# Two-layer transformer kernel: self key scores without mask products, GpSimd zeroing of unseen exponentials, value products in halves between pairs of score steps

## What is computed

```python
w = jnp.einsum('bhqd,bhkd->bhqk', q, k) / jnp.sqrt(jnp.asarray(HD, q.dtype))
if causal_bool:                      # self attention
    mask = jnp.tril(jnp.ones((ql, kl), bool))
    w = jnp.where(mask[None, None], w, neg)
if tril_diag2_additive:              # cross attention: two keys further are seen
    cm = jnp.tril(jnp.ones((ql, kl), w.dtype), k=2)
    w = w + jnp.where(cm == 0, neg, jnp.zeros((), w.dtype))[None, None]
if extra_bias is not None:
    w = w + extra_bias[:, None, None, :]
w = jax.nn.softmax(w, axis=-1)
return jnp.einsum('bhqk,bhkd->bhqd', w, v)
```

## Time and profile before

| | |
|---|---|
| median of 3 runs | 1627.18 us (1626.68 to 1628.8) |
| the profiled execution's own time | 1632.07 us |
| its span | 1630.3 us |
| TensorE busy | 1429.8 us (88%) |
| VectorE busy | 1114.9 us (68%) |
| ScalarE busy | 987.3 us (61%) |
| GpSimd busy | 317.8 us (19%) |
| mean granted TensorE clock | 0.956 |

### The profile page before, as it was taken

One profiled execution on the slowest core, in us unless ns is written; L12 is line 12 of the kernel. 1 busy time (PEld: TensorE's weight loads), 2 busy tenths in 40 slices (PEclk: granted clock), 3 DMA queues, 4 the chain that ended last, 5 costly groups with the idle time before them and its releaser, 6 DMA issues. The chain is left out here.

```text
span 1630.3 us, 39092 instructions
## 1 busy us (share of the span) xinstructions
PE 1429.8 (88%) x15448; PEld 877.1 (54%) x15448; DVE 1114.9 (68%) x3252; ACT 987.3 (61%) x1618; POOL 317.8 (19%) x428
## 2 busy tenths in 40 slices
PE   2667799989899999989899999989899998989887
PEld 1445565655656465555646565555656565555442
DVE  5556676786777677777777677677767667646344
ACT  2254666675757576675757567585757666572642
POOL 3421211121212121121212111121212102020120
PEclk7587899999999999999999999999999999997998
DMA  3324111213040312213040222203031211010000
GB/s 70 57 74 58 44 33 39 38 32 50 12 71 10 54 29 38 38 25 57 10 73 10 46 30 38 45 19 63 10 62 21 38 32 35 2 32 5 14 7 7
DMA packets 79214, 58.05 MB, mean 36 GB/s; under 512 B 11004, under 2 KB 78902, under 8 KB 79030
## 3 DMA queue, kind: packets, MB, share of 16 engines
q1 hardware_dynamic: 76726, 53.90, 18.9%
q10 hardware_dynamic: 2304, 1.64, 0.7%
HBM read 11.57 MB, written 4.19 MB: 10 GB/s over the span
## 5 line engine op out<-in xcount | busy, mean ns | idle before, releaser
L1025 DVE TENSOR_REDUCE chunkmax<-ps 128x3 f32<-128x384 f32 (+1 forms) x1024 | 507.8, 553 | 116.7 <-PE ps L1379 111.1
L711 ACT ACTIVATE probs<-ps 128x768 f32<-128x768 f32 (+1 forms) x512 | 405.6, 808 | 183.5 <-PE ps L1374 179.8
L1444 PE MATMUL ps<-zT,w 128*128 128x512 f32 x576 | 281.5, 603 | 6.9 <-ACT silu_a L728 5.2
L728 ACT ACTIVATE silu_a<-ps,b 128x512 f32<-128x512 f32 x144 | 98.7, 685 | 198.2 <-PE ps L1444 174.8
L1359 PE MATMUL ps<-k_op,q_op 48*128 48x256 bf16 x512 | 145.2, 286 | 52.0 <-DVE chunkmax L1025 38.2
L1166 DVE SCALAR_TENSOR_TENSOR h_open<-ps,b,silu_a 128x512 f32<-128x512 f32 x128 | 95.7, 748 | 124.0 <-PE ps L1444 113.5
L1341 PE MATMUL ps<-q_op,k_op 51*128 51x256 bf16 x512 | 143.4, 280 | 27.1 <-DMA xq_op<-xq_parts 9.1
L1444 PEld LDWEIGHTS ps<-zT,w 128*128 128x128 f32 x576 | 103.0, 192 | 114.5 <-issue 87.3
L1480 PE MATMUL ps<-hT,w 128*128 128x512 f32 x288 | 149.5, 600 | 3.8 <-DVE hT L1172 3.0
L1359 PE MATMUL ps<-xk_op,xq_op 51*128 51x256 bf16 x512 | 145.3, 285 | 5.1 <-DVE chunkmax L1025 4.8
L1371 PE MATMUL ps<-xmask_q_lo,ident_lo 64*128 64x262 bf16 x512 | 145.1, 285 | 0.0
(11 more groups left out here) (245 smaller groups left out, 3436.4 us busy)
## 6 DMA issues: line engine op xcount, KB each, us to landing
q_op<-q_parts SPq DMA_DIRECT2D x192, 64.0 KB
xq_op<-xq_parts SPq DMA_DIRECT2D x192, 64.0 KB
k_op<-k_parts SPq DMA_DIRECT2D x168, 64.0 KB
x_tm<-in_L_attn_hidden_states SPq DMA_DIRECT2D x16, 256.0 KB, 6.0
x_keep<-in_L_attn_hidden_states SPq DMA_DIRECT2D x16, 256.0 KB, 6.1
out<-o_tm SPq DMA_DIRECT2D x16, 256.0 KB, 2.3
k_op<-k_parts ACTq DMA_DIRECT2D x24, 64.0 KB
w<-in_L_ffn_rw SPq DMA_DIRECT2D x1, 1024.0 KB
```

The costliest lines, as they stand in the source:

```text
L711: act.activation(probs[:, four % 2, 2 * pair:2 * pair + 2, 0:T + a.seen], ps[:, 2 * (1 - g % 2):2 * (1 - g % 2) + 2, 0:T + a.seen], ACT.Ex ...
L1025: dve.tensor_reduce(chunkmax[:, b, at, :], ps[:, MAX_BANK[n], 0:3 * a.seen].rearrange("p (c n) -> p c n", c=3), AX.X, ALU.max).then_inc(a. ...
L1444: pe.matmul(ps[:, bank, :], w, src[:], start=True, stop=True).then_inc(sig.sem, 1)
```

## The change

The self attention's key scores get no mask products any more (`first_keys`, `second_keys`; `a.selects` is true for the self attention). Behind each exponential GpSimd sets the unseen entries of its 128x(2x2x128) block to zero (`keep_seen`, `affine_select` in place) and raises a new semaphore `kept`, for which the value products of the self attention wait in place of `exp`. `probs` gets a third buffer, used by the self attention only, so its value products may come one group later. To make room, three weight tiles of the setup now lie in `geluT`.

A value group is cut into its two halves. In the self phase two steps are written out together (`two_steps`), and a half follows every second step: the first half of group g behind step 4g+9, its second half behind step 4g+11. Groups 6 and 7 come when all steps are done. In the cross phase `score_step` stays, the first half of group g comes behind step 4g+6 and the second behind step 4g+8, and groups 6 and 7 come at the end. The query scores that run beside self key scores use banks 6, 7, 5 until step 23, banks 6 and 7 for steps 24 to 27, and 4, 6, 7 from step 28 (`WITH_SELF`). By the rule (4, 6, 7)[n % 3] steps 28 and 29 fall into banks 6 and 7 too. ScalarE copies the first context half behind exponential 11 in place of 10 in the self phase.

```diff
-        mask_k_lo = sb("mask_k_lo", [128, 2, 64], BF16)
-        mask_k_hi = sb("mask_k_hi", [128, 256], BF16)
...
-        probs = sb("probs", [128, 2, 4, T + XW])
+        probs = sb("probs", [128, 3, 4, T + XW])
...
+        wxq0, wxk, wxkv = geluT[:, 3, 0:D], geluT[:, 3, D:2 * D], geluT[:, 3, 2 * D:4 * D]
...
+            a.selects = not cross
+            a.kept = signal(n + "_kept", H)
+            a.buffers = 2 if cross else 3
...
+        def max_banks(shared, own):
+            n_5, n_4 = shared, own
+            return [(6, 7, 5)[n % 3] for n in range(n_5)] + [(6, 7)[n % 2] for n in range(n_5, n_4)] \
+                + [(4, 6, 7)[n % 3] for n in range(n_4, 2 * H)]
+        WITH_SELF, WITH_CROSS = max_banks(24, 28), max_banks(20, 24)
+        def banks_for(a, j):
+            return WITH_SELF if a.cross or j < 2 else WITH_CROSS
...
-                for m in (mask_k_lo, mask_k_hi, xmask_q_lo, xmask_q_hi, xmask_k_lo, xmask_k_hi, pick):
+                for m in (xmask_q_lo, xmask_q_hi, xmask_k_lo, xmask_k_hi, pick):
...
-                    select(mask_k_lo[p], ALU.is_ge, MASKED, 0, [[0, 2], [1, 64]], -1)
-                    select(mask_k_hi[p], ALU.is_ge, MASKED, -HALF, [[0, 2], [1, 128]], -1)
...
+            def keep_seen(a, j, first, last):
+                for g in range(first, last):
+                    four, pair = divmod(g, 2)
+                    late_and_early = probs[:, four % a.buffers, 2 * pair:2 * pair + 2, 0:2 * a.seen]
+                    pool.wait_ge(*a.exp.part(j, g + 1))
+                    pool.affine_select(out=late_and_early, in_=late_and_early, compare_op=ALU.is_ge, fill=0.0, base=0,
+                                       pattern=[[0, 2], [0, 2], [1, a.seen]],
+                                       channel_multiplier=-1).then_inc(a.kept.sem, 1)
             def body(i, par):
                 k = i - 2
 
+                if exists(i):
+                    keep_seen(sa, i, 0, 2)
                 if exists(k):
 
                     pool.wait_ge(*n_mlp.out.done(k))
                     add_bias(h2b, h2, bmlp, ca.h.done(k), h3_sb.before(k), h2b_ready)
+                if exists(i):
+                    keep_seen(sa, i, 2, H)
...
-                    act.wait_ge(*(a.pv.part(j, four - 1) if four >= 2 else used_before))
+                    act.wait_ge(*(a.pv.part(j, four + 1 - a.buffers) if four >= a.buffers else used_before))
...
-                    if g == 10:
+                    if g == (10 if a.cross else 11):
...
+            def first_keys(a, j, par, m):
+                kt, qt, h2, k0, q0 = key_operands(a, par, m)
+                if m % 2 == 0 and m >= 4:
+                    pe.wait_ge(*a.exp.part(j, m // 2 - 1))
+                pe.matmul(bank_of(m)[:, a.seen:a.seen + T], kt[:, h2, k0:k0 + 128], qt[:, h2, q0:q0 + T],
+                          start=True, stop=False, skip_group_check=True)
+            def second_keys(a, j, par, m):
+                kt, qt, h2, k0, q0 = key_operands(a, par, m)
+                last = pe.matmul(bank_of(m)[:, 0:a.seen], kt[:, h2, k0 + 128:k0 + T], qt[:, h2, q0 + T - a.seen:q0 + T],
+                                 start=False, stop=a.selects, skip_group_check=True)
+                if a.selects and m % 2:
+                    last.then_inc(a.st_ps.sem, 1)
...
+                if keys and not a.selects:
+                    first_key_mask(a, m)
...
+            def two_steps(a, j, par, other, jo, paro, n, free_4, free_5):
+                first_keys(a, j, par, n)
+                late_queries(a, j, other, jo, paro, n, free_4, free_5)
+                second_keys(a, j, par, n)
+                early_queries(other, jo, paro, n)
+                late_queries(a, j, other, jo, paro, n + 1, free_4, free_5)
+                late_query_mask(other, jo, n)
+                early_queries(other, jo, paro, n + 1)
+                early_query_mask(other, jo, n)
+                first_keys(a, j, par, n + 1)
+                late_query_mask(other, jo, n + 1)
+                second_keys(a, j, par, n + 1)
+                early_query_mask(other, jo, n + 1)
...
+            def value_half(a, four, half, j, par):
 
                 s, b, aa = four // 4, four // 2 % 2, four % 2
-                pe.wait_ge(*a.exp.part(j, 2 * four + 2))
+                if half == 0:
+                    pe.wait_ge(*(a.kept if a.selects else a.exp).part(j, 2 * four + 2))
                 late = T - a.seen
                 bank = ps[:, 4 + s, :]
-                for half in range(2):
-                    for jj in range(4):
-                        h = 8 * s + 4 * aa + jj
-                        v = xv_st[:, half, h, :] if a.cross else v_st[:, par, 2 * b + half, h, :]
-                        q0 = b * T + (late if half else 0)
-                        last = pe.matmul(bank[32 * jj:32 * jj + 32, q0:(b + 1) * T], v,
-                                         probs[:, four % 2, jj, (0 if half else a.seen):(a.seen if half else a.seen + T)],
-                                         start=(aa == 0 and half == 0), stop=(aa == 1 and half == 1),
-                                         skip_group_check=True)
-                last.then_inc(a.pv.sem, 1)
+                for jj in range(4):
+                    h = 8 * s + 4 * aa + jj
+                    v = xv_st[:, half, h, :] if a.cross else v_st[:, par, 2 * b + half, h, :]
+                    q0 = b * T + (late if half else 0)
+                    last = pe.matmul(bank[32 * jj:32 * jj + 32, q0:(b + 1) * T], v,
+                                     probs[:, four % a.buffers, jj, (0 if half else a.seen):(a.seen if half else a.seen + T)],
+                                     start=(aa == 0 and half == 0), stop=(aa == 1 and half == 1),
+                                     skip_group_check=True)
+                if half:
+                    last.then_inc(a.pv.sem, 1)
+            def values_behind(a, j, par, other, jo, step, free_4, free_5):
+                four, at = divmod(step, 4)
+                lag = a.buffers - 1
+                first, second = (1, 3) if a.selects else (2, 4)
+                if at == second % 4 and four >= lag + second // 4:
+                    value_half(a, four - lag - second // 4, 1, j, par)
+                if at == first and lag <= four < 6 + lag:
+                    if four == lag:
+                        free_4()
+                    if four == 4 + lag:
+                        free_5()
+                        if exists(jo):
+                            pe.wait_ge(*other.s_max.part(jo, last_in_5(banks_for(other, jo)) + 1))
+                    value_half(a, four - lag, 0, j, par)
...
-                for four in range(8):
-                    for step in range(4 * four, 4 * four + 4):
-                        if step == 2:
-                            free_01()
+                for step in range(2 * H):
+                    if step == 2:
+                        free_01()
+                    if not (exists(j, jo) and a.selects):
                         score_step(a, j, par, step, other, jo, paro, step, free_4, free_5)
-                    if exists(j) and four:
-                        if four == 1:
-                            free_4()
-                        if four == 5:
-                            free_5()
-                            if exists(jo):
-                                pe.wait_ge(*other.s_max.part(jo, LAST_IN_5 + 1))
-                        value_group(a, four - 1, j, par)
+                    elif step % 2 == 0:
+                        two_steps(a, j, par, other, jo, paro, step, free_4, free_5)
+                    if exists(j):
+                        values_behind(a, j, par, other, jo, step, free_4, free_5)
                 if exists(j):
-                    value_group(a, 7, j, par)
+                    for four in (6, 7):
+                        value_half(a, four, 0, j, par)
+                        value_half(a, four, 1, j, par)
```

More of the change, by code:

```diff
@@ new lines, in second_key_mask, with query_operands @@
+            def second_key_mask(a, m):
+                own = slice(HALF * (1 - m % 2), HALF * (1 - m % 2) + HALF)
+                last = pe.matmul(bank_of(m)[:, 0:2 * a.seen].rearrange("p (c n) -> p c n", c=2)[:, :, 0:64], ident_lo[own],
+                                 a.mk_lo[own], start=False, stop=True, skip_group_check=True)
+                if m % 2:
+                    last.then_inc(a.st_ps.sem, 1)
+            def query_operands(other, paro, n):
+                b, h = divmod(n, H)
+                hh = h % 2
+                ks, qs = k_rows(other, paro, hh, other.rows_s), q_rows(other, paro, hh, other.rows_s)
+                return ks[:, h // 2], qs[:, h // 2], 0 if other.cross else b * T, b * T
@@ L1327, in score_step, with early_query_mask @@
+            def early_query_mask(other, jo, n):
+                own = slice(HALF * (n % 2), HALF * (n % 2) + HALF)
+                ch = other.seen
```

(3 more changed lines are left out.)

109 lines of the change are left out of this document (50 added, 59 removed).

## The result

The changed kernel takes 1654.01 us (median, 1651.12 to 1655.45) where the kernel before takes 1627.99 us beside it. The ratio is 1.0155, 95% interval 1.014 to 1.017: slower by 1.6%, where 1618.9 us was forecast. The profiled execution has a span of 1649.4 us against 1630.3.

A forecast was written before the change was run, and what follows sets the result against it. TensorE and VectorE were taken to bound the self loop together, ScalarE the cross phase's end. Gains of 2.1 + 1.1 + 1.1 + 4.0 = 8.3 us gave 1618.9 us on the median, range 1592 to 1640.

The forecast's parts named there:

- Part 4: Cross phase: dividing value groups taken as 0, from -0.7 to +0.5 us per phase.
- nothing changes: Rival: cross-phase halves, +0.5 us each phase, eat the setup and self-phase gains; 1626 us, chance 0.06.
- One sign of being wrong: Profile after: exponentials that hold the value halves of the cross phase; no size given.
- Part 3: Self phase: waits at `mlp_input`, `h2b`, two-bank steps and last select leave a gain of about 0.25 us, 4.0 over 16.
- the beat: Self phase: four score steps with their value halves go from 2.40 to 2.11 us where nothing else holds them.
- my second rival: Last select isn't repaid: select and semaphore add 0.85 us to each self phase; 1636.5 us, chance 0.14.
- Part 1: Self key scores without mask products: two steps take 0.52 us instead of 0.69, 2.7 per phase if nothing else waited.
- Part 2: Value halves: wide 0.52, narrow 0.26 us, each plus entry 0.09; VectorE idle 0.14 once in four steps.
- The two-bank steps: Self steps 26 to 29: VectorE waits 0.50 us twice, giving back most of the lead.
- Part 5: Setup and start: first self phase 2.1 us earlier, then 1.1 in it and 1.1 in the second and third together.
- The other rivals: Beat takes hold in both phases, 1592 us (0.25); slow select, 1681 (0.08); clock falls, near 1660 (0.05).
- the rival's 3.6 us per phase: Slow select: fourteen selects at 1.22 us end at 593.7 rather than 589.95, 3.6 us per self phase; chance 0.08.

The follow-up runs named there:

- e1: Changed kernel with whole value groups in the cross phase, placed as before; 1631.41 us, ratio 1.0025.
- e2: Changed kernel with the cross halves one step later, behind steps 4g+7 and 4g+9; 1630.78 us, ratio 1.0027.
- e10: e1 with its whole cross value groups behind step 4g+6, between the two steps of one exponential; 1672.02 us, ratio 1.0284.
- e9: e5 with the self phase's score steps one by one instead of in interleaved pairs; 1611.89 us, ratio 0.9909.
- e4: Kernel before without its two self key mask products, unseen keys not masked; 1619.16 us, ratio 0.9959.
- e6: e1 with whole value groups in the self phase too; 1644.03 us, ratio 1.0091.
- e5: e1 with the last pair of self key steps, 30 and 31, masked by products, so exponential 15 needs no select; 1621.29 us, ratio 0.9956.
- e3: Changed kernel without GpSimd's selects, unseen exponentials not zeroed; 1635.85 us, ratio 1.0051.
- e11: e5 with selects 2 and 3 ahead of GpSimd's sum h2b; 1620.38 us, ratio 0.9956.
- e7: e5 and e6 together: no divided value group, last self key pair masked by products; 1635.61 us, ratio 1.004.
- e12: e9 and e11 together; 1606.83 us, ratio 0.9878.
- e13: Changed kernel with only its self steps one by one instead of in pairs; 1641.63 us, ratio 1.0072.

## Why the prediction was wrong

The direction was wrong and the range missed. Its sum had -8.3 us on the profiled execution, the spans show +19.1.

- **Part 4, the cross phase taken as 0, is the step that failed.** It cost 0.76 us in each full phase, 3.6 and 5.7 in the last two (2 to 3 of the 5.7 by the clock, below), and 21.8 in all sixteen. I had weighed the halves against TensorE's beat and VectorE's reserve, and written that "the end is ScalarE's" as if that protected the phase. It is the reverse: since ScalarE ends this phase, the 0.58 us lost at exponential 3 were never caught up. The diff shows both halves behind an even step (4g+6 and 4g+8), between the two that one exponential waits for; I saw where the first lands among the maxima and did not ask the exponentials. e1, e2 and e10 show it. The rival "nothing changes" had +0.5 per phase. One sign of being wrong did name exponentials and value halves, but the other way round (exponentials that hold the halves), and without a price.
- **The last two cross phases were not looked at.** Without query steps ScalarE has next to no slack: before, it is busy 16.78 of 16.80 us in the last but one and 15.37 of 16.40 in the last. The ScalarE timelines of the last but one, before and after:

```profile
1433.49 3.02 ACT L711 ACTIVATE probs<-ps 128x772 f32<-128x772 f32 x4
1436.40 1.63 ACT L689 ACTIVATE h<-h,tiny_post 128x128 f32<-128x128 f32 x4
1437.94 3.00 ACT L711 ACTIVATE probs<-ps 128x772 f32<-128x772 f32 x4
```

```profile
1444.14 2.32 ACT L734 ACTIVATE probs<-ps 128x772 f32<-128x772 f32 x3
1447.32 0.81 ACT L734 ACTIVATE probs<-ps 128x772 f32<-128x772 f32 x1 [0.87 <-PE ps L1385]
...
1449.57 1.49 ACT L734 ACTIVATE probs<-ps 128x772 f32<-128x772 f32 x2
1451.82 0.81 ACT L734 ACTIVATE probs<-ps 128x772 f32<-128x772 f32 x1 [0.75 <-PE ps L1385]
```

  Strings of four exponentials are broken by 0.75 to 0.87 us, several times a phase.
- **Part 3, the last select not repaid.** The select measured 0.637 (0.63 forecast), TensorE's wait for it 0.74 and its whole cost 0.78 (0.7 forecast). But the maxima, from the first one's start to the last one's end, gained 0.6 instead of 0.93, and the last exponential 0.46 instead of 0.90. With 0.16 before the phase, an iteration has +0.16 instead of -0.25, some 6.6 us over sixteen. Counted from the first maximum, maximum 10 starts at 6.83 (6.78 forecast, as before), maximum 24 at 14.61 (14.41 forecast), and the last ends at 19.79 (19.46 forecast). So the mis-sized terms are the beat (below) and the steps behind maximum 24; the pair order costs the first maxima another 0.22, by e9's 6.61, which I had not looked for. This is my second rival at its deciding point (0.6 us); e1 alone, at 1631.4, lies between it and the forecast.
- **Part 1, a step's slots.** Two steps with an entry are 0.61 us, as forecast. What I credited to the interleaved order belongs to the missing masks: single steps have the same 0.61 (e9). By e4 the missing masks give 0.34 us per self phase by themselves, far below the 2.7 of the slots, and that value groups and `mlp_input` still hold the beat, as part 3 had it, is the likely reason; no run takes it apart.
- **Part 2, the halves.** Right in the self phase: VectorE's idle stretch is 0.18 (e9; 0.14 forecast), and dividing gains 0.88 per phase (e6). From its start to the next step a half takes 0.57 (wide, 608.84 to 609.41 above) and 0.36 (narrow, 577.70 to 578.06 in e5), where two thirds and one third of 0.78 gave 0.52 and 0.26. A wide half with two steps is then 1.18 us on TensorE against 1.00 for two maxima, and 2.00 with 0.18 idle are the beat of 2.19, where the forecast had 1.97 and 0.14.
- **Part 3, the waits.** Group 1 waited for select 3 behind `h2b`: right, 0.23 us (e3, e11). The two-bank steps: 0.44 twice for 0.50 twice. I had named them as a cost of `two_steps` and not gone on to ask what the pairs give in return; the answer is nothing.
- **Part 5, the start.** 1.9 us were gained by the fourth self phase while the first two cross phases had already lost 2.2, some 4.1 together. The forecast has 4.3 for the start and 0.75 for three self phases. Its parts were off: the first key step started 1.1 us earlier, not 2.1. The trace puts its wait down to a transfer in place of GpSimd's last select:

```profile
74.91 0.37 PE L1365 MATMUL ps<-q_op,k_op 51*128 51x256 bf16 x1 [8.20 <-DMA q_op<-maxT]
```

- **The other rivals.** No select was slow (the rival's 3.6 us per phase should read 3.75, 593.7 less 589.95). The Trainium skill, GPSIMD Engine Reference, section Performance versus the Vector engine, has 2.6 cycles per element at 1.2 GHz for work with two inputs, which as an estimate gave 1.11 us; the 0.637 measured for one input does not follow it. From the fourth iteration on the clock held at 1.00 in the full phases but one, a cross phase of 24.04 us at 0.93. Busy time by stretch with the columns of the earlier trace rows, self phase, cross phase and the last two cross phases:

```profile
571.50:591.30 19.80, 17.74 (x296) 9.02 (x294) 16.95 (x34) 14.65 (x21) 10.64 (x17) 1.00 0.33 46
605.40:628.80 23.40, 20.22 (x354) 11.26 (x350) 20.29 (x61) 18.93 (x33) 8.64 (x12) 1.00 0.04 13
1444.10:1464.50 20.40, 16.80 (x232) 8.51 (x226) 4.31 (x25) 17.05 (x30) 6.13 (x8) 1.00 0.05 15
1529.90:1552.00 22.10, 19.75 (x224) 9.48 (x224) 1.49 (x11) 15.94 (x26) 4.79 (x6) 0.77 0.08 25
```

  In the last cross phase the clock did fall. The same phase before, in e3 (cross phases as in the changed kernel), in e7 and in e10:

```profile
1516.60:1533.00 16.40, 13.44 (x224) 7.73 (x224) 1.49 (x11) 15.37 (x26) 4.83 (x6) 0.90 0.12 34
1515.70:1540.00 24.30, 23.28 (x220) 10.78 (x224) 1.49 (x11) 16.03 (x26) 4.80 (x6) 0.56 0.08 23
1521.50:1537.40 15.90, 12.15 (x224) 7.05 (x224) 1.49 (x11) 15.39 (x26) 4.82 (x6) 1.00 0.11 34
1540.00:1569.20 29.20, 25.35 (x224) 13.01 (x224) 1.49 (x11) 15.72 (x26) 4.78 (x6) 0.53 0.06 19
```

  At 1.00 this phase is 0.9 us shorter than the one before it (15.87 and 16.81 in e7). By that, as an estimate, the changed kernel's would be 19.5 at full clock, so 2 to 3 of its 22.13 us are the clock's.

The self phase set one edit against another. From e4 (19.81 us, masks gone, nothing else), dividing the groups takes 0.88 away, the pairs add 0.45 and the selects inside 0.23: 19.61, and 19.69 was measured. The last select adds 0.78 behind it. Keeping what gains (no masks, divided self groups, selects) and dropping what costs (pairs, cross halves, the last select, the place behind `h2b`) is e12.

## What to carry to other kernels

Before work is put between two steps, list everything that waits for both of them, on every engine: halves of 0.57 and 0.36 us between the two steps of one exponential cost 21 us over the run, the same halves one step later 0 to 5. Ask first which engine ends the phase, and for each of its instructions what it waits for. And where a chain of producers ends a phase, the last piece can be made in the old way: 30 of 32 steps took the cheap mask, and two kept the products, because there the select had nothing to hide behind.

## What the runs showed of the hardware

- A GpSimd select of 512 float32 elements on 128 partitions took 637 ns in place (256 of them, median 637, 637 to 716), beside busy VectorE and ScalarE.
- Two parts of a float32 value group hold the next step back by 0.57 us (1024 columns) and 0.36 us (512 columns), the whole by 0.78 (1536 columns). All three fit 0.15 us and 0.21 per 512 columns, so dividing a group costs one 0.15 more.
- In the last cross phase the granted clock was 0.77 (0.90 in the same phase before) while TensorE counted as busy 19.75 of 22.10 us, that is, a part of it at the level of 1.2 GHz. The same cross products took 22.13 us at 0.77, and 24.37 (e3) and 24.35 (e13) at 0.56. In e10 that phase took 29.24 us at 0.53 against 21.09 at 1.00 for the one before it. In the kernels with nothing between an exponential's two steps it is 0.90 or 1.00 and the phase at most 17.20. Why it falls lower when TensorE's work is spread over a longer phase, these runs do not settle.
